# Rest of the layer: four of twelve norms scaled by VectorE, the fp8 overflow test in one operation, and the pieces of the four batches in another order

## The chip, the cores and the metric

The kernel runs on one core of a Trainium2 chip. The metric is the device time of one execution in microseconds; the median of several runs counts. TensorE does matmuls and transposes, VectorE and GpSimd elementwise work and reductions, ScalarE activations and copies, SyncE issues the transfers. Each engine works through its own list of instructions in the order in which it is written, and waits at semaphores.

## What is computed

One decoder layer on `x` (4 batches, 512 positions, 128 features) with a context of 77 rows. Each of three parts is added to its input and normalised:

```python
x = _layernorm(x + attn(x, Wq, Wk, Wv, bq, bk, bv, Wo, bo))       # causal, 16 heads of 64
x = _layernorm(x + xattn(x, ctx_1024, ctx_1024, Wq, Wk, Wv, Wo))  # 16 heads of 8, 77 keys
x = _layernorm(x + ffn(x, kernel, input_scale, kernel_scale, bias))
# _layernorm: (x - mean) / sqrt(var + 1e-5); ffn: x to bf16, / s_in, to float8_e4m3fn, one 128x128 matmul
```

In `float8_e4m3fn` a value that rounds to more than 448 becomes NaN. The kernel does this rounding in fp32 by hand.

## The kernel before

`self_attention` does the causal attention of all heads up to the product with Wo. It takes the first 319 us and is the same before and after. `rest_of_layer` does everything behind it, in pieces. A piece is a small function with a batch number, and each engine has its part of it under the same name. A piece's TensorE part fills a bank (or two banks) of PSUM, and another engine takes the result out:

- `y(b)`: attention times Wo, 32 matmuls. VectorE adds the input (`add(1, b)`) and takes mean and variance (`stats(1, b)`); then comes the norm.
- `t(b)`, `q(b)`: the normed batch transposed, and the queries from it; ScalarE copies both out, VectorE makes the low half (`q_lo`).
- `m(b, k)`, k from 0 to 7: scores in the other orientation, of which VectorE takes the maxima (tile `top`, line 850). `r(b)` transposes these maxima, ScalarE copies them to `shift`.
- `s(b, k)`, k from 0 to 3: the shifted scores of four heads, 16 matmuls into two places; ScalarE takes the exponentials in two halves (tile `p_t`, line 694, half 0 and then half 1).
- `p(b, part)`: exponentials times values, 8 matmuls (16 in the trace, which shows two passes for fp32). `o(b, part)`: transpose; VectorE divides (`o_n`). `u(b)`: transpose back. `z(b)`: times Wo.
- `add(2, b)`, `stats(2, b)`, norm; `cast(b)` on ScalarE (bf16, scale); `fp8(b)` on VectorE (rounding, `quant`); `x(b)`, `f(b)`: transpose and the feed-forward matmul; `add(3, b)`, `stats(3, b)`, norm, and SyncE stores the batch.

`s(1, 2)` is written s(1,2) below, and so on. `norm(l, b)` of GpSimd has two steps: the power -0.5 of the variance (tile `rstd`, line 755) and four scalings of 128x128 (line 758).

PSUM is shared by table `USES`: places n0 and n1 are one bank each, x0, x1 and x2 two banks each. The table lists for each place the pieces that use it, in order. `claim` lets TensorE start a piece only when the place's previous user has been taken. A piece `s(b,k)` needs two of the three x places; half 0 of its exponentials frees the first of them, half 1 the second. The order of the pieces on each engine is written out by hand, as a list of calls, in each engine's block. So TensorE, too, holds everything behind a piece that waits.

Of the kernel before, what the change touches and what calls it, by code (L numbers as in the profile page):

```python
# [440 lines left out]
def rest_of_layer(nc, banks, attn_t, consts, consts_in, x_nat, out):  # L441
# [7 lines left out]
    with ctx:  # L449
# [72 lines left out]
        @block.tensor
        def _(pe):
# [138 lines left out]
            x(1); f(1); x(2); f(2); x(3); f(3)

        @block.scalar
        def _(act):
# [71 lines left out]
            t(0); q(0); t(1); q(1); r(0); t(2); q(2); s(0, 0, 0); s(0, 0, 1); s(0, 1, 0); s(0, 1, 1); r(1); t(3)  # L737
            p(0, 0); s(0, 2, 0); s(0, 2, 1); q(3); s(0, 3, 0); s(0, 3, 1); s(1, 0, 0); s(1, 0, 1); p(0, 1)
            s(1, 1, 0); s(1, 1, 1); r(2); s(1, 2, 0); s(1, 2, 1); p(1, 0); s(2, 0, 0); s(2, 0, 1); u(0); s(1, 3, 0)
            s(1, 3, 1); s(2, 1, 0); p(1, 1); s(2, 1, 1); cast(0); u(1); s(2, 2, 0); r(3); s(2, 2, 1); p(2, 0)  # L740
            s(3, 0, 0); s(3, 0, 1); x(0); s(2, 3, 0); s(2, 3, 1); f(0); s(3, 1, 0); p(2, 1); cast(1); s(3, 1, 1)
# [229 lines left out]
```

## Time and profile before

| | us |
|---|---|
| median of 3 runs | 483.58 (483.56 to 483.71) |
| profiled execution | 480.95 |
| its span, first to last instruction | 479.2 |
| busy in the span: TensorE, VectorE, ScalarE, GpSimd | 413.8, 307.9, 254.3, 248.1 |
| granted clock of TensorE, mean | 0.932 |

The profiled execution is 2.6 us shorter than the median of the timed runs. Times inside the trace count from the start of the span. A granted clock of 1.00 is 2.4 GHz, 0.50 is 1.2 GHz, and a mean between them mixes the two. The share of busy time is over the whole span; the part that is changed begins at 319 us.

### The profile page before, as it was taken

The page shows a single profiled execution, that of the slowest core. Times are in us where ns is not written, and L with a number is a line of the kernel's source. Part 1 is how long each engine was busy: PE and PEld are TensorE (multiplying, and loading weights), DVE is VectorE, ACT ScalarE, POOL GpSimd, SP SyncE. Part 2 cuts the span into 40 slices and gives each one's busy share as a digit, 9 for nine tenths or more (in the row PEclk, how much of TensorE's full clock was granted, in tenths as well). Part 3 has the DMA queues.
Part 4 walks back from the last instruction along what each step waited for, and adds up shares of the span by engine and source line. Part 5 has one row for each costly group of instructions (what it writes and reads, how often), then busy time and mean ns, then how long its engine had stood idle before and what let it go on. Part 6 is the DMA issues. An engine that isn't in the chain of part 4 may idle for free. (4 is left out here: it accounts for less than half of the span.)

```text
span 479.2 us, 10059 instructions
## 1 busy us (share of the span) xinstructions
PE 413.8 (86%) x3954; PEld 291.1 (61%) x3954; DVE 307.9 (64%) x901; ACT 254.3 (53%) x370; POOL 248.1 (52%) x318
## 2 busy tenths in 40 slices
PE   3789999999999999999999999867998798787500
PEld 1576776777777677677677777547974334344200
DVE  1558878777877777877877777344248433566772
ACT  2266666667667667666766756511011447755410
POOL 2377856556646646655655664645642000335277
PEclk9899999999999999999999999999996679977955
DMA  7300000000000000000000000020000000000001
GB/s 248 98 2 1 1 3 1 2 1 1 1 2 3 0 2 4 0 1 1 2 1 1 3 1 1 1 83 6 1 2 0 1 0 1 1 0 23 1 22 45
DMA packets 4559, 6.89 MB, mean 14 GB/s; under 512 B 1440, under 2 KB 2976, under 8 KB 4384
## 3 DMA queue, kind: packets, MB, share of 16 engines
q1 hardware_dynamic: 4512, 6.24, 4.0%
q8 instruction: 32, 0.52, 0.5%
q14 instruction: 15, 0.12, 0.1%
HBM read 5.19 MB, written 1.05 MB: 13 GB/s over the span
## 5 line engine op out<-in xcount | busy, mean ns | idle before, releaser
L312 DVE CUSTOM_DVE_ANT_0 unused<-banks,neg_mask 128x512 bf16<-128x512 f32 (+3 forms) x256 | 112.6, 487 | 43.1 <-PE banks L108 43.0
L255 ACT ACTIVATE probs<-banks 128x768 f32<-128x768 f32 (+1 forms) x96 | 84.9, 884 | 56.5 <-PE banks L129 56.5
L370 POOL TENSOR_SCALAR_AFFINE_SELECT probs<-probs 128x256 f32<-128x256 f32 x128 | 50.5, 407 | 110.4 <-ACT probs L255 107.6
L158 PE MATMUL banks<-probs,v_nat 128*64 128x256 f32 (+3 forms) x512 | 74.4, 432 | 0.0
L158 PEld LDWEIGHTS banks<-probs,v_nat 128*64 128x64 f32 x512 | 37.0, 137 | 45.5 <-issue 40.4
L388 POOL TENSOR_TENSOR p_sum<-probs 128x768 f32<-128x768 f32 x32 | 58.6, 1830 | 2.7
L755 POOL TENSOR_TENSOR rstd<-var_e,halves 128x4 f32<-128x4 f32 x12 | 12.4, 1038 | 90.0 <-DVE var_e L834 90.0
L124 PE MATMUL banks<-q_hi,k_hi 64*128 64x512 f32 (+3 forms) x256 | 45.9, 354 | 2.9 <-ACT probs L255 2.9
L129 PE MATMUL banks<-shift,ones_r 64*128 64x512 f32 (+3 forms) x256 | 45.2, 348 | 0.0
L321 DVE SCALAR_TENSOR_TENSOR q_lo<-banks,bias_qk,q_hi 128x512 fp32r<-128x512 f32 x32 | 24.0, 751 | 29.6 <-ACT q_hi L277 29.6
L395 POOL TENSOR_TENSOR p_sum<-p_sum,probs 128x512 f32<-128x512 f32 x32 | 40.9, 1277 | 2.7
L124 PE MATMUL banks<-q_lo,k_hi 64*128 64x512 f32 (+3 forms) x256 | 41.6, 320 | 0.0
L124 PE MATMUL banks<-q_hi,k_lo 64*128 64x512 f32 (+3 forms) x256 | 41.5, 319 | 0.0
L261 ACT CAST shift<-banks 128x512 fp32r<-128x512 f32 x32 | 18.8, 587 | 40.0 <-PE banks L138 40.0
L108 PE MATMUL banks<-k_hi,q_hi 64*128 64x512 f32 (+3 forms) x256 | 37.3, 326 | 1.7 <-DMA attn_t<-w_qkv 1.7
L694 ACT ACTIVATE p_t<-banks 77x1024 f32<-77x1024 f32 x32 | 31.2, 1018 | 13.2 <-PE banks L606 13.2
L850 DVE TENSOR_REDUCE top<-banks 128x8 f32<-128x616 f32 x32 | 24.2, 795 | 19.2 <-PE banks L587 18.9
L200 PE MATMUL banks<-x_hi,w_hi 64*128 64x512 f32 x128 | 27.1, 417 | 7.1 <-POOL neg_max L402 6.2
L566 PE MATMUL banks<-wo_s,attn_t 128*128 128x128 f32 x256 | 29.4, 276 | 3.3 <-POOL vx L777 2.5
L338 DVE TENSOR_TENSOR banks<-banks,r_near 128x512 f32<-128x512 f32 x32 | 22.4, 700 | 14.4 <-ACT r_near L287 10.7
L129 PEld LDWEIGHTS banks<-shift,ones_r 64*128 64x128 f32 x256 | 24.4, 186 | 11.7 <-ACT shift L261 11.7
L566 PEld LDWEIGHTS banks<-wo_s,attn_t 128*128 128x128 f32 x256 | 28.8, 192 | 3.9 <-issue 2.7
(121 smaller groups left out, 881.1 us busy)
## 6 DMA issues: line engine op xcount, KB each, us to landing
attn_t<-w_qkv SPq DMA_DIRECT2D x1, 1344.0 KB, 8.1
attn_t<-xT SPq DMA_DIRECT2D x4, 256.0 KB, 8.5
x_s<-x_nat SPq DMA_DIRECT2D x1, 1024.0 KB, 5.8
out<-y_out SPq DMA_DIRECT2D x4, 256.0 KB, 2.0
...
```

Source lines behind the costliest of these rows:

```text
L108: last = mm(mx[:, h, at:at + n], q_hi[HALF[h], v % 3, i * T:(i + 1) * T], k_hi[HALF[h], v % 3, 0:n], start=True, stop=True)
L124: mm(st[:, h, at:at + n], k[HALF[h], par, ks], q[HALF[h], par, j * T:S], start=(c == 0), stop=False)
L129: last = mm(st[:, h, at:at + n], ones_r[HALF[h], :], shift[HALF[h], v % 2, j * T:S], start=False, stop=True)
L158: last = mm(o_ps[HALF[h], j * T:S], v_nat[:, v // 2 % 2, j, v % 2, HALF[h]], p_of(v, j, h, 0, S - j * T), start=(j == 0), stop=(j == NT - 1))
L200: last = mm(aux[qk], w[HALF[h], qk, p, :], x[HALF[h], xs], start=(part == 0 and c == 0), stop=(part == 1 and c == 2))
L255: nc.scalar.activation(probs[:, v % 2, AT[j]:AT[j] + 2 * n].rearrange("p (h s) -> p h s", h=2), st[:, :, 0:n], ACT.Exp, scale=D ** -0.5).t ...
L312: last = V.tensor_tensor_reduce(out=unused[:, h, at:at + n], in0=mx[:, h, at:at + n], in1=neg_mask[:, S - n:S], scale=-1.0, scalar=3.0e38, ...
L370: return nc.gpsimd.affine_select(out=blk, in_=blk, compare_op=ALU.is_ge, fill=0.0, base=0, pattern=pattern + [[1, T]], channel_multiplier=-1)
L388: nc.gpsimd.tensor_tensor(acc[:, :, :], heads(0, T, S), heads(1, 0, S - T), ALU.add).then_inc(added, 1)
L395: nc.gpsimd.tensor_tensor(acc[:, :, T:], acc[:, :, T:], heads(2, 0, 2 * T), ALU.add).then_inc(added, 1)
L566: last = mm(dst[:, i * T:(i + 1) * T], attn_t[:, p, at:at + T], wo_s[:, p, :], start=(p == 0), stop=(p == PAIRS - 1))
L694: nc.scalar.activation(p_t[:, k, 2 * half:2 * half + 2, :], place[bank][0:C, :, :], ACT.Exp, scale=DK ** -0.5).then_inc(taken[bank], 1)
```

## The change

Three edits, all in `rest_of_layer`.

1. The norm is split into `power(l, b)`, which stays on GpSimd, and `scale(l, b)`. Four of the twelve scalings, (1,0), (2,3), (3,2) and (3,3), are done by VectorE in the same form, four operations of 128x128; eight stay on GpSimd. Waits for a normed batch now ask the semaphore of the engine that scaled it.
2. `rounding` tested for overflow with three operations (square, compare and scale, scale to infinity times zero). Now one operation scales the value by 7.2e35 and multiplies by zero, which is NaN where the value was 480 or more. Each `fp8(b)` has six VectorE operations instead of eight.
3. The table of PSUM places and the lists of calls of all engines are in a new order.

```diff
 USES = {
-    "x0": "k m00 m03 m05 m11 m14 m17 m20 s01 m24 s02 m27 m31 m32 s11 m34 s20 s13 s21 s30 s23 s32 s33",
-    "x1": "v m01 m04 m07 m13 m16 s00 m21 m23 s02 s03 m30 s10 m33 s12 m35 s13 m37 s22 s23 s31 s33",
-    "x2": "m02 m10 m06 m12 m15 s00 s01 m22 m25 m26 s03 s10 s11 s12 s20 m36 s21 s22 s30 s31 s32",
+    "x0": "k m01 m04 m07 m14 m20 s00 m23 s01 m25 s03 m27 s11 m31 s13 s20 s21 m36 s22 s30 s31 s33",
+    "x1": "v m02 m05 m10 m12 m15 m21 m22 m17 m24 s02 m26 s10 m30 s12 s13 s20 m35 m37 s23 s30 s32 s33",
+    "x2": "m00 m03 m06 m11 m13 m16 s00 s01 s02 s03 s10 s11 s12 m32 m33 m34 s21 s22 s23 s31 s32",
 }
...
+        SCALED = {"pool": "11 12 13 20 21 22 30 31".split(), "dve": "10 23 32 33".split()}
...
+        def wait_scaled(eng, l, b):
+
+            by = "pool" if f"{l}{b}" in SCALED["pool"] else "dve"
+            eng.wait_ge(scaled[by], SCALED[by].index(f"{l}{b}") + 1)
...
-            norm(1, 0); norm(1, 1); norm(1, 2); norm(1, 3); norm(2, 0); norm(2, 1); norm(3, 0); norm(2, 2)
-            norm(2, 3); norm(3, 1); norm(3, 2); norm(3, 3)
+            power(1, 0); power(1, 1); scale(1, 1); power(1, 2); scale(1, 2); power(1, 3); scale(1, 3); power(2, 0)
+            scale(2, 0); power(2, 1); scale(2, 1); power(2, 2); scale(2, 2); power(3, 0); scale(3, 0); power(2, 3)
+            power(3, 1); scale(3, 1); power(3, 2); power(3, 3)
...
-                    lambda: V.tensor_tensor(m, v, v, ALU.mult),
-                    lambda: V.tensor_scalar(m, m, 448.0 ** 2, 3.0e38, ALU.is_gt, ALU.mult),
-                    lambda: V.tensor_scalar(m, m, 3.0e38, 0.0, ALU.mult, ALU.mult))
+                    lambda: V.tensor_scalar(m, v, 7.2e35, 0.0, ALU.mult, ALU.mult))
...
+            def scale(l, b):
+
+                dve.wait_ge(pow_out, POWS.index(f"{l}{b}") + 1)
+                for i in range(NT):
+                    last = V.tensor_scalar((y_out if l == 3 else xn)[:, b, i, :], r_s[:, b, i, :], mv[:, b, i, 0:1],
+                                           rstd[:, b, i:i + 1], ALU.subtract, ALU.mult)
+                last.then_inc(dve_scaled, 1)
```

In TensorE's list `y(3)` stood ahead of `q(0)` and all `m`; now `t(0)`, `t(1)`, `q(0)` and the first five `m` of batch 0 stand ahead of it. The next place is TensorE from the fourth part of `s(0,0)` on. The old list reads s(0,0) m(2,0) s(0,1) m(2,1) r(1) m(2,2) m(2,3) m(2,4) m(2,5) p(0,0) s(0,2); line 606 is `s`, 587 is `m`, 537 with `top` is `r`, 617 is `p`. Before, from the end of s(0,1):

```order
L606 MATMUL banks<-shift,neg_sel 77x512 x4
L587 MATMUL banks<-kx_hi,q_hi 128x308 x2
L537 MATMUL banks<-ident_f_s,top 128x128 x4
L587 MATMUL banks<-kx_hi,q_hi 128x308 x8
L617 MATMUL banks<-p_t,vx 32x512 x8
L606 MATMUL banks<-q_hi,kx_hi 77x512 x4
```

Now, at the same place; line 615 is `s`, 596 `m`, 546 with `top` is `r`, 626 is `p`:

```order
L615 MATMUL banks<-shift,neg_sel 77x512 x4
L596 MATMUL banks<-kx_hi,q_hi 128x308 x2
L546 MATMUL banks<-ident_f_s,top 128x128 x4
L615 MATMUL banks<-q_hi,kx_hi 77x512 x4
L615 MATMUL banks<-q_lo,kx_hi 77x512 x4
L615 MATMUL banks<-q_hi,kx_lo 77x512 x4
L615 MATMUL banks<-shift,neg_sel 77x512 x4
L596 MATMUL banks<-kx_hi,q_hi 128x308 x2
L626 MATMUL banks<-p_t,vx 32x512 x8
L615 MATMUL banks<-q_hi,kx_hi 77x512 x4
```

Between s(0,1) and s(0,2) there were five `m`, `r(1)` and `p(0,0)`; now there are one `m` and `r(1)`, and `p(0,0)` stands behind s(0,2).

The other place is VectorE at its end. The first rows are `add(2,3)` and `stats(2,3)`, then `add(3,1)`. Before:

```order
L816 TENSOR_TENSOR r_s<-banks,xn 128x512
L827 BN_STATS stats<-r_s 128x6 x4
L831 BN_AGGR mv<-stats 128x2 x4
L834 TENSOR_SCALAR var_e<-mv 128x4
L806 TENSOR_TENSOR xq<-y_b,ffn_b_s 128x512
L810 TENSOR_TENSOR r_s<-xq,xn 128x512
L827 BN_STATS stats<-r_s 128x6 x4
L831 BN_AGGR mv<-stats 128x2 x4
L834 TENSOR_SCALAR var_e<-mv 128x4
L806 TENSOR_TENSOR xq<-y_b,ffn_b_s 128x512
L810 TENSOR_TENSOR r_s<-xq,xn 128x512
L790 TENSOR_SCALAR qm<-qv 128x512
```

Now:

```order
L825 TENSOR_TENSOR r_s<-banks,xn 128x512
L836 BN_STATS stats<-r_s 128x6 x4
L840 BN_AGGR mv<-stats 128x2 x4
L843 TENSOR_SCALAR var_e<-mv 128x4
L815 TENSOR_TENSOR xq<-y_b,ffn_b_s 128x512
L819 TENSOR_TENSOR r_s<-xq,xn 128x512
L849 TENSOR_SCALAR xn<-r_s,mv,rstd 128x128 x4
L836 BN_STATS stats<-r_s 128x6 x4
L840 BN_AGGR mv<-stats 128x2 x4
L843 TENSOR_SCALAR var_e<-mv 128x4
L801 TENSOR_SCALAR qm<-qv 128x512
```

`scale(2,3)` (line 849) is new behind `add(3,1)`, and `add(3,2)` has moved behind `fp8(3)`. The last eight VectorE operations are now `scale(3,2)` and `scale(3,3)`.

## Rows read from the trace of the kernel before

**Rows 1.** The page's slices of the span: TensorE busy, and its granted clock.

```profile
PE   3789999999999999999999999867998798787500
...
PEclk9899999999999999999999999999996679977955
```

**Rows 2.** Stretches: us, busy time (instructions) of each engine, granted clock, DMA.

```profile
357.50:372.30 14.80, 12.57 (x51) 6.15 (x50) 12.61 (x23) 2.38 (x5) 4.15 (x5) 0.68 0.00 0
372.30:394.00 21.70, 17.68 (x117) 8.21 (x116) 9.13 (x13) 10.34 (x13) 0.00 (x0) 0.67 0.00 1
394.00:408.80 14.80, 13.04 (x146) 7.20 (x150) 6.56 (x12) 11.06 (x14) 0.00 (x0) 1.00 0.01 1
408.80:424.70 15.90, 13.34 (x106) 6.23 (x106) 8.08 (x21) 9.48 (x13) 4.16 (x5) 0.79 0.00 1
424.70:452.60 27.90, 19.88 (x168) 10.34 (x165) 18.98 (x55) 15.76 (x22) 13.41 (x15) 0.88 0.03 11
```

**Rows 3.** TensorE in order of time: start, us, line, operation [idle before, releaser].

```profile
333.32 14.53 PE L566 MATMUL banks<-wo_s,attn_t 128*128 128x128 f32 x128 [2.45 <-POOL vx L777]
...
348.63 7.41 PE L566 MATMUL banks<-wo_s,attn_t 128*128 128x128 f32 x64 [0.34 <-DVE r_s L816]
...
381.52 3.64 PE L617 MATMUL banks<-p_t,vx 77*32 77x512 f32 x16
385.09 0.71 PE L606 MATMUL banks<-q_hi,kx_hi 32*77 32x512 f32 x4
...
395.36 1.92 PE L617 MATMUL banks<-p_t,vx 77*32 77x512 f32 x16
397.36 0.47 PE L606 MATMUL banks<-q_hi,kx_hi 32*77 32x512 f32 x4
...
400.61 0.46 PE L606 MATMUL banks<-q_hi,kx_hi 32*77 32x512 f32 x4 [1.37 <-ACT p_t L694]
...
439.87 0.71 PE L606 MATMUL banks<-q_hi,kx_hi 32*77 32x512 f32 x4
...
449.38 1.16 PE L539 MATMUL banks<-w_x_s,on_t 128*128 128x128 f32 x8 [0.73 <-ACT on_t L671]
```

**Rows 4.** VectorE in order of time, the same columns.

```profile
358.21 7.15 DVE L850 TENSOR_REDUCE top<-banks 128x8 f32<-128x616 f32 x10
...
439.98 0.69 DVE L816 TENSOR_TENSOR r_s<-banks,xn 128x512 f32<-128x512 f32 x1 [1.65 <-PE banks L539]
...
452.60 0.68 DVE L816 TENSOR_TENSOR r_s<-banks,xn 128x512 f32<-128x512 f32 x1
...
461.23 0.43 DVE L790 TENSOR_SCALAR qm<-qv 128x512 int32<-128x512 int32 x1 [2.80 <-ACT qv L714]
...
463.87 0.82 DVE L794 TENSOR_TENSOR qm<-qv 128x512 f32<-128x512 f32 x1
...
465.65 0.69 DVE L877 TENSOR_TENSOR xq<-qv,qm 128x512 bf16<-128x512 f32 x1
...
469.17 0.51 DVE L806 TENSOR_TENSOR xq<-y_b,ffn_b_s 128x512 bf16<-128x512 bf16 x1 [1.43 <-ACT y_b L725]
...
471.81 0.18 DVE L834 TENSOR_SCALAR var_e<-mv 128x4 f32<-128x4 f32 x1
```

**Rows 5.** GpSimd in order of time, at the end.

```profile
456.13 3.67 POOL L758 TENSOR_SCALAR xn<-r_s,mv,rstd 128x128 f32<-128x128 f32 x4
...
472.56 1.02 POOL L755 TENSOR_TENSOR rstd<-var_e,halves 128x4 f32<-128x4 f32 x1
473.69 3.12 POOL L758 TENSOR_SCALAR y_out<-r_s,mv,rstd 128x128 f32<-128x128 f32 x4
```

**Rows 6.** ScalarE in order of time: two exponentials, and the last cast.

```profile
398.54 1.93 ACT L694 ACTIVATE p_t<-banks 77x1024 f32<-77x1024 f32 x2 [0.61 <-PE banks L606]
...
459.83 0.62 ACT L712 CAST x_b<-xn 128x512 bf16<-128x512 f32 x1 [3.24 <-POOL xn L758]
```

**Rows 7.** Tile qv: durations in ns, first and last start, form.

```profile
L790 DVE TENSOR_SCALAR qm<-qv x1: 227/227/227, 322.7 to 322.7; 128x128 int32<-128x128 int32 x1
```

More of the change, by code:

```diff
@@ L707, in cast @@
             def cast(b):
-                act.wait_ge(norm_out, norm_at(2, b) + 1)
+                wait_scaled(act, 2, b)
                 if b:
@@ L735, in _ @@
             act.wait_ge(prep, 2)
[L737 to L741, printed above, removed]
-            u(2); s(3, 2, 0); s(3, 2, 1); s(3, 3, 0); s(3, 3, 1); p(3, 0); p(3, 1); cast(2); u(3); x(1); f(1); x(2)
-            f(2); cast(3); x(3); f(3)
+            t(0); q(0); t(1); q(1); t(2); q(2); r(0); t(3); s(0, 0, 0); s(0, 0, 1); s(0, 1, 0); s(0, 1, 1); r(1)
+            s(0, 2, 0); s(0, 2, 1); p(0, 0); s(0, 3, 0); s(0, 3, 1); q(3); s(1, 0, 0); s(1, 0, 1); p(0, 1)
+            s(1, 1, 0); s(1, 1, 1); r(2); s(1, 2, 0); s(1, 2, 1); p(1, 0); u(0); s(1, 3, 0); s(1, 3, 1); s(2, 0, 0)
+            s(2, 0, 1); p(1, 1); s(2, 1, 0); s(2, 1, 1); cast(0); u(1); s(2, 2, 0); s(2, 2, 1); r(3); s(2, 3, 0)
+            s(2, 3, 1); p(2, 0); s(3, 0, 0); s(3, 0, 1); p(2, 1); cast(1); s(3, 1, 0); s(3, 1, 1); u(2); s(3, 2, 0)
+            x(0); s(3, 2, 1); s(3, 3, 0); s(3, 3, 1); p(3, 0); f(0); p(3, 1); cast(2); x(1); u(3); f(1); x(2); f(2)
+            cast(3); x(3); f(3)
         @block.gpsimd
@@ L749, in _, with power @@
             values = v2_s[:, :, :].rearrange("k b (t a d) -> k (b t) a d", t=8, a=2)
-            def norm(l, b):
-                n = norm_at(l, b)
-                pool.wait_ge(var_out, n + 1)
+            def power(l, b):
+                pool.wait_ge(var_out, norm_at(l, b) + 1)
                 P.tensor_tensor(rstd[:, b, :], var_e[:, b, :], halves[:, :], ALU.pow).then_inc(pow_out, 1)
-                pool.wait_ge(pow_out, n + 1)
+            def scale(l, b):
+                pool.wait_ge(pow_out, POWS.index(f"{l}{b}") + 1)
                 for i in range(NT):
@@ L759, in norm @@
                                            rstd[:, b, i:i + 1], ALU.subtract, ALU.mult)
-                last.then_inc(norm_out, 1)
+                last.then_inc(pool_scaled, 1)
             P.memset(halves[:, :], -0.5).then_inc(zeroed, 1)
@@ L834, in stats, with scale @@
                 V.tensor_scalar(var_e[:, b, :], mv[:, b, :, 1], EPS, None, ALU.add).then_inc(var_out, 1)
+            def scale(l, b):
+                dve.wait_ge(pow_out, POWS.index(f"{l}{b}") + 1)
[3 more added lines that the diff above has]
+                last.then_inc(dve_scaled, 1)
             def q(b):
@@ L899, in _ @@
             dve.wait_ge(zeroed, 2)
-            add(1, 0); stats(1, 0); add(1, 1); stats(1, 1); add(1, 2); stats(1, 2); add(1, 3); stats(1, 3); m(0, 0)
-            m(0, 1); m(0, 2); m(0, 3); m(1, 0); m(0, 4); m(0, 5); m(0, 6); m(0, 7); m(1, 1); q(0); m(1, 2); m(1, 3)
-            q(1); m(1, 4); m(1, 5); m(1, 6); m(1, 7); m(2, 0); q(2); m(2, 1); m(2, 2); m(2, 3); m(2, 4); m(2, 5)
-            m(2, 6); q(3); m(2, 7); m(3, 0); m(3, 1); o(0, 0); m(3, 2); m(3, 3); o(0, 1); m(3, 4); m(3, 5); o(1, 0)
-            m(3, 6); add(2, 0); stats(2, 0); m(3, 7); o(1, 1); fp8(0); add(2, 1); stats(2, 1); o(2, 0); add(3, 0)
-            stats(3, 0); o(2, 1); fp8(1); add(2, 2); stats(2, 2); o(3, 0); o(3, 1); fp8(2); add(2, 3); stats(2, 3)
-            add(3, 1); stats(3, 1); add(3, 2); fp8(3); stats(3, 2); add(3, 3); stats(3, 3)
+            add(1, 0); stats(1, 0); scale(1, 0); add(1, 1); stats(1, 1); add(1, 2); stats(1, 2); m(0, 0); m(0, 1)
+            m(0, 2); m(0, 3); m(0, 4); q(0); add(1, 3); stats(1, 3); m(0, 5); m(0, 6); m(1, 0); q(1); m(1, 1)
+            m(0, 7); m(1, 2); m(1, 3); m(1, 4); m(1, 5); m(2, 0); m(1, 6); q(2); m(2, 1); m(2, 2); m(2, 3); m(1, 7)
+            m(2, 4); m(2, 5); m(2, 6); o(0, 0); m(2, 7); q(3); m(3, 0); m(3, 1); o(0, 1); m(3, 2); m(3, 3)
+            add(2, 0); stats(2, 0); m(3, 4); o(1, 0); m(3, 5); o(1, 1); m(3, 6); m(3, 7); fp8(0); add(2, 1)
+            stats(2, 1); o(2, 0); o(2, 1); fp8(1); add(2, 2); stats(2, 2); add(3, 0); o(3, 0); stats(3, 0); o(3, 1)
+            fp8(2); add(2, 3); stats(2, 3); add(3, 1); scale(2, 3); stats(3, 1); fp8(3); add(3, 2); stats(3, 2)
+            add(3, 3); stats(3, 3); scale(3, 2); scale(3, 3)
 _INS = ["xT", "w_qkv", "b_qk", "b_v", "causal", "ident", "x_nat", "wo", "b_o", "ctx_t", "w_x", "row_mask",
```

30 lines of the change are left out of this document (16 added, 14 removed), and 4 rows, old and new, of the table USES.

## The prediction

> **What bounds the kernel now.** I read the page first, then stretches, then each engine in order of time. The page's slices [rows 1] show TensorE at nine tenths and a granted clock of 0.9 or more for the first 30 slices. Behind them both become ragged, and the last two slices have no TensorE work. So the changed part has two regimes: a middle, up to the last `z`, and a tail, in which one batch runs alone through all engines.
>
> The stretches [rows 2] say what holds the middle. From 357.5 to 372.3 VectorE is busy 12.61 of 14.80 us: it takes the maxima of `m`, 10 in 7.15 us, 0.72 each [rows 4]. From 372.3 no engine is full, except that TensorE looks busy, 17.68 of 21.70, at a granted clock of 0.67. At 1.00 (394.0 to 408.8) the same kind of work moves quickly. Two things therefore cost time here: pieces in the order in which they stand in a queue, and the low clock. The low level is dear: a `p` took 3.64 us at 381.5 and 1.92 us at 395.4 [rows 3].
>
> In the tail, read backwards [rows 4 to 6]: the last variance is ready at 471.99 (471.81 + 0.18), but GpSimd is still scaling batch 2 and starts its power at 472.56. The last scaling begins at 473.69. Before that, 3.67 us of GpSimd scaling of (2,3) from 456.13 stand directly in front of the cast at 459.83, and VectorE's `fp8(3)`, started at 461.23, ends at 466.34.
>
> **The change: the tail.** I count from the start of `add(2,3)`, 452.60, to the end of the span, 479.2: 26.6 us.
>
> - `scale(2,3)` on VectorE. No row shows this operation at this size with two scalars from memory. The nearest is a VectorE operation of 128x128 with constants, 0.227 us alone [rows 7]; four of them one behind another give 0.9 at most, and by the same row somewhat less if they overlap, as the ten `top` operations do. The upper bound is GpSimd's 3.67 [rows 5]. The operation is of VectorE's kind, so I take 0.75. It stands behind `add(3,1)` (about 1.2), which is as long as the power (1.02 and a hand-off) that it waits for. Saving: 3.67 - 0.75 = 2.9. Range of this term: 0 to 3.1.
> - `stats(3,1)` stands behind it, about 1.5, beside cast and scale on ScalarE (459.83 to 461.23, 1.4). It costs 0.1 or 0.2.
> - Overflow test. Three operations from 463.87 to 465.65, 1.78 us, become one of 0.46. Saving 1.3. The other three `fp8` save the same, behind which `add(2,1)`, `add(2,2)` and `add(2,3)` stand on VectorE; that is in the middle's count.
> - From the end of `fp8(3)` through `x(3)` and `f(3)` to 469.17 nothing changes, 2.8 us. `add(3,2)` and `stats(3,2)`, about 2.8 together, now fill just this gap; if they are longer by a few tenths, so is the tail.
> - The last norm. Before: 471.99 to 476.81 (473.69 + 3.12), 4.8 us. Now GpSimd has only powers left: 1.1 with its hand-off, during which VectorE does `scale(3,2)`, then `scale(3,3)`, 0.75. With hand-offs 2.0. Saving 2.8.
>
> Sum: -2.9 + 0.1 - 1.3 - 2.8 = **-6.9** us, a tail of 19.7.
>
> **The change: the middle.** From 333.3, where `y(1)` starts [rows 3], to 452.60 it lasts 119.3 us. I walked through the new lists with durations at full clock (`y` 7.3 us, `s` 1.2, `p` 1.9, `z` 1.2, a maximum 0.72, two exponentials 1.93 [rows 3, 4, 6]), each piece starting when its place is free, its input there and its queue at it. The checkpoints, before and in my walk (the stretches of rows 2 are cut at the starts of s(0,0), s(1,0) and s(2,1)):
>
> - `s(0,0)` starts at 372.3; 371.4. `y(3)` is 7.4 us of pure TensorE work [rows 3], and it now starts about 4.6 us later, at 353.2, behind five `m`. VectorE, which was idle during `y(3)`, takes five maxima (3.6 us) in that time, then `add(1,3)` and `stats(1,3)` (2.3). Both ways VectorE has done about 4.4 us of this work by 360.5, so the exchange is near zero by itself. From there it has 11 maxima and one `q_lo` to do: 360.5 + 2.3 + 7.9 + 0.7 = 371.4.
> - `s(1,0)` starts at 394.0; 384.8. A step from one `s` to the next that shares the place freed last is the matmuls, 1.18 (397.36 to the exponentials at 398.54), then both exponentials, 1.93: with hand-offs 3.24 us, as from 397.36 to 400.61 [rows 3, 6]. One that shares the place freed first saves one exponential, about 2.3. New table: four steps of 3.2 to 3.5, 13.4 us, where the trace has 21.7. The reason is in the queue: s(0,2) stood behind `p(0,0)` and five `m` and started at 385.09. VectorE and ScalarE waited meanwhile, and the clock was low.
> - `s(2,1)` starts at 408.8; 402.9. Here 3.3 us go back, since `p(1,1)` is now ahead of it (before, behind it).
> - `s(3,3)` starts at 439.87; 423.3. Steps of 3.8, 3.3, 3.0, 4.4, 3.6, 2.3. Before, TensorE here twice waited behind ScalarE, which waited for a GpSimd scaling ahead of a `cast`, and lost its clock twice. In my walk `cast(0)` finds its batch ready, at 405.6, before ScalarE comes to it.
> - `add(2,3)` starts at 452.60; 435.9. `z(3)` ends near 434.8 (at 450.5 before: 449.38 + 1.16), and `fp8(2)`, one us later, decides.
>
> At full clock this is -16.7. It is too good by two amounts. The walk leaves out hand-offs of some 0.1 us where two engines finish together: I add 1.5. And it assumes the clock. Before, rows 2 show means of 0.68, 0.67, 0.79 and 0.88. With two levels, 1.00 and 0.50, that is (1 - mean)/0.5 of each stretch at the low one: 9.5, 14.3, 6.7 and 6.7, together 37 us. TensorE is busy for 0.8 of it, and low clock takes 0.47 of such time (1.92 instead of 3.64 for a `p`): 14 us at most. I take 12, since VectorE's maxima cover part of the first. The low passages came behind ones in which TensorE was idle or half idle. Its work in rows 2 is 76.5 us in 95.1, at full clock 64; the walk puts it, with 3 us of `y(3)`, into 78 us, so a share of 0.86 instead of 0.67. But it has the same VectorE-bound passage before s(0,0), three-microsecond steps with single `m` between them, and a thin end around `u(3)`, `z(3)`. I expect half of the loss to remain, 6 us. Middle: -16.7 + 1.5 + 6 = **-9.2**.
>
> On this the page "TensorE: Matmul & The Clock Gate", section "A second HAM failure mode: psum-queue depth-cycling", speaks against the change. By that section of the Trainium skill, a TensorE that idles briefly between groups while PSUM places are cycled makes its clock swing again and again. Place x2 is used by seven `s` in a row, so by that rule the loss would remain whole. Against it, this trace kept 1.00 from 394.0 to 408.8 [rows 2] in steps of 3.3 us with the same wait at each.
>
> **Sum.** -6.9 - 9.2 = -16.1. The profiled execution, 480.95, would be 464.8; its distance to the median (2.6) kept, 467.4: I say 467.4.
>
> **The rivals.**
>
> - A, chance 0.50: as above. Its own range is 463.5 to 471.5, half to nearly all of the clock loss either way and 1 us for the scaling term.
> - B, 0.17: the clock falls as often as before. TensorE work at 1.2 GHz costs the full 12: 467.4 + 6 = 473.4. For it speaks the same VectorE-bound stretch, against it the denser queue.
> - C, 0.18: the clock holds nearly throughout: 467.4 - 6 = 461.4. For it speaks 394.0 to 408.8, against it the mean of 0.79 right behind.
> - D, 0.09: the new order gives nothing, since what s(0,2) gains is given back at `cast` and `fp8` (the two chains per batch take the time that they take). Then only the tail counts: 483.6 - 6.9 = 476.7. Against it: the last of these chains, batch 2's, began at 439.98 with `add(2,2)`, which had waited 1.65 us for `z(2)` of TensorE [rows 4], at low clock.
> - E, 0.03, slower: TensorE stays at 1.2 GHz from `y(3)` on. It has to wait there for the maxima of the first `m`, and before, the clock fell in just such a passage (357.5 to 372.3, 0.68). `y(3)` would take 7 us more. The 54 us of TensorE work behind s(0,0) (63.9 by rows 2, less its share of the 12) would take 1.7 times as long, 92 us where the walk has 64: 28 more. With C's 461.4 that is 496. It decides once low clock costs more than 22 us, that is for some 50 of these 64. Before, the low passages of rows 2 added up to 28 of 80.
> - F, 0.03: a cancelling mix within 0.2%, which is about what a measurement of this kernel can tell from no change.
>
> **How the numbers follow.** The range 460 to 475 holds A, B and C almost whole, 0.82 with their outer edges cut; D and E lie outside. Faster by over 0.2% is A, B, C and D, 0.94; same 0.03; slower 0.03. If the VectorE scaling were as slow as GpSimd's, A would be at 472, still inside.
>
> **What would show it.** VectorE's four scalings of a batch at 0.6 to 0.9 us together, no L794 to L796 work but one operation of 0.43, `fp8(3)` at 3.5 to 3.9 us. A span of about 463, in it from `add(2,3)` to the end 19 to 20.5 us. s(0,0) at 371 to 375, s(0,2) within 7.5 us behind it, s(3,3) near 427, `add(2,3)` near 443. The mean granted clock over 357 to 443 above 0.80, with passages at 0.50 after thin ones. I am wrong if s(0,0) is later than 376 (then moving `y(3)` cost something), if steps between `s` exceed 4 us on average from s(0,0) to s(3,3), or if the tail is over 22.

## The result, and the profile after

The changed kernel takes 463.63 us (median of 4 runs, 458.4 to 467.37) against 483.57 for the kernel before; the ratio is 0.9566, 95% interval 0.9475 to 0.9657. In a second comparison it was 461.76 us (7 runs) and 0.9516 (0.9461 to 0.9571). The forecast was 467.4 in a range of 460 to 475. The profiled execution of the changed kernel is one of its longer ones, 467.37 us, and the comparison of the ratio leaves such executions out; I therefore read a second trace as well (trace 2, 467.75 us), and show where the length comes from.

The stretches of the changed kernel, columns as in [rows 2]:

```profile
357.50:372.30 14.80, 13.13 (x91) 9.57 (x91) 9.58 (x21) 1.68 (x3) 5.75 (x8) 0.94 0.00 1
372.30:394.00 21.70, 18.22 (x122) 8.66 (x118) 10.38 (x16) 9.95 (x14) 0.00 (x0) 0.66 0.00 1
394.00:408.80 14.80, 13.18 (x124) 6.70 (x125) 5.41 (x9) 9.52 (x14) 0.00 (x0) 0.87 0.00 1
408.80:424.70 15.90, 14.66 (x160) 7.31 (x162) 11.93 (x35) 12.71 (x17) 5.78 (x7) 1.00 0.00 1
424.70:439.00 14.30, 11.82 (x124) 5.92 (x116) 8.58 (x24) 10.81 (x15) 6.24 (x8) 1.00 0.01 1
439.00:465.60 26.60, 7.26 (x44) 4.76 (x40) 22.47 (x79) 7.50 (x12) 15.02 (x15) 0.56 0.11 41
```

Against [rows 2] the low clock is gone from 408.8 to 439.0. It is still there from 372 to 394, 0.66 where it was 0.67, and from 394.0 to 408.8 the clock is 0.87 where it was 1.00. In the last stretch TensorE works for 7 us only.

TensorE in order of time, columns as in [rows 3]: `y(3)`, s(0,0), s(0,1), s(0,2), p(0,0), s(1,0) and s(3,3).

```profile
357.86 7.41 PE L575 MATMUL banks<-wo_s,attn_t 128*128 128x128 f32 x64
...
376.87 0.46 PE L615 MATMUL banks<-q_hi,kx_hi 32*77 32x512 f32 x4 [0.18 <-DVE top L867]
...
380.43 0.56 PE L615 MATMUL banks<-q_hi,kx_hi 32*77 32x512 f32 x4 [0.64 <-DVE top L867]
...
384.37 0.71 PE L615 MATMUL banks<-q_hi,kx_hi 32*77 32x512 f32 x4 [0.81 <-ACT p_t L703]
...
386.56 3.64 PE L626 MATMUL banks<-p_t,vx 77*32 77x512 f32 x16
...
394.23 0.71 PE L615 MATMUL banks<-q_hi,kx_hi 32*77 32x512 f32 x4 [0.81 <-ACT p_t L703]
...
433.04 0.47 PE L615 MATMUL banks<-q_hi,kx_hi 32*77 32x512 f32 x4 [0.16 <-ACT p_t L703]
```

s(0,2) now comes 3.94 us behind s(0,1). `p(0,0)` follows it and still pays the low clock, 3.64 us.

VectorE in the tail, columns as in [rows 4]: `add(2,3)`, `scale(2,3)`, first and last operation of `fp8(3)` with the new test (line 805) between them, `add(3,3)`, and the last two scalings, `scale(3,2)` and `scale(3,3)`. Then GpSimd's last two powers.

```profile
445.66 0.69 DVE L825 TENSOR_TENSOR r_s<-banks,xn 128x512 f32<-128x512 f32 x1
...
449.12 1.11 DVE L849 TENSOR_SCALAR xn<-r_s,mv,rstd 128x128 f32<-128x128 f32 x4 [0.20 <-POOL rstd L762]
...
451.67 0.43 DVE L801 TENSOR_SCALAR qm<-qv 128x512 int32<-128x512 int32 x1
...
454.18 0.56 DVE L805 TENSOR_SCALAR qm<-qv 128x512 f32<-128x512 f32 x1
454.78 0.69 DVE L894 TENSOR_TENSOR xq<-qv,qm 128x512 bf16<-128x512 f32 x1
...
458.29 0.43 DVE L815 TENSOR_TENSOR xq<-y_b,ffn_b_s 128x512 bf16<-128x512 bf16 x1 [0.18 <-ACT y_b L734]
...
460.87 2.35 DVE L849 TENSOR_SCALAR y_out<-r_s,mv,rstd 128x128 f32<-128x128 f32 x8
```

```profile
458.19 1.03 POOL L762 TENSOR_TENSOR rstd<-var_e,halves 128x4 f32<-128x4 f32 x1 [0.94 <-DVE var_e L843]
461.04 1.03 POOL L762 TENSOR_TENSOR rstd<-var_e,halves 128x4 f32<-128x4 f32 x1 [1.82 <-DVE var_e L843]
```

The scaling of (2,3) takes 1.11 us where GpSimd took 3.67 [rows 5]. GpSimd is free for the last power at once, and the scalings end at 463.2, 2.25 us behind the last variance at 460.97; before it was 4.8.

All traces are compared by one table. Each number is the us between two starts read from the two timelines: t(0), s(0,0), s(1,0), s(2,1), s(3,3), `add(2,3)`, and the end of the span. The walk is that of the prediction, all at 1.00. The names of the other versions are those of the experiments below.

```
                    t00-s00  s00-s10  s10-s21  s21-s33  s33-add23  tail   span
before                24.6     21.8     14.7     31.1     12.7     26.6   479.2
walk                  23.7     13.4     18.1     20.4     12.6     19.7   455.6
changed, trace 1      24.6     17.4     18.6     20.2     12.6     19.9   465.6
changed, trace 2      28.8     18.6     17.2     20.2     12.8     20.0   465.0
order only            24.6     14.2     17.2     22.1     14.4     26.8   466.4
scalings only         24.6     21.7     14.7     31.1     12.7     22.4   476.1
fp8 test only         24.6     21.8     14.7     31.1     11.5     25.4   476.5
y3_early              32.5     18.6     20.5     20.2     12.5     20.0   471.8
p_ahead               24.7     18.0     17.2     20.2     12.5     20.0   461.6
m_twice               26.9     16.2     17.7     20.2     12.8     20.0   466.6
m_twice_early         27.0     15.8     17.2     20.2     12.5     20.0   465.1
filler_one            27.6     16.3     17.6     20.2     12.4     20.0   467.0
filler_two            31.2     14.7     17.9     20.2     12.5     20.0   465.3
filler_bf16           29.9     18.7     22.6     20.2     12.4     19.9   476.9
filler_bf16_late      29.1     14.7     17.4     20.2     12.4     19.9   464.0
```

The three columns from s(2,1) to the end repeat to 0.4 us in all versions with the new order and both other edits; what varies lies ahead of s(2,1). The granted clock varies there too: between s(0,0) and s(1,0) it is 0.67 before, 0.61 and 0.54 in the two traces of the changed kernel, 0.88 in order_only and 0.72 in p_ahead.

### The profile page after: what moved, and what is told of

Read it like the earlier page. It is cut to its first block and busy times, and to the rows that moved or that the text cites. A ratio compares the mean times of both kernels' runs of the same rounds, so it can differ in the third digit from the quotient of the medians.

```text
span 465.6 us, 10048 instructions
## 1 busy us (share of the span) xinstructions
PE 412.6 (89%) x3954; PEld 291.8 (63%) x3954; DVE 307.1 (66%) x907; ACT 253.9 (55%) x370; POOL 236.8 (51%) x302
## 5 line engine op out<-in xcount | busy, mean ns | idle before, releaser
L158 PE MATMUL banks<-probs,v_nat 128*64 128x256 f32 (+3 forms) x512 | 75.8, 438 | 0.0
L108 PE MATMUL banks<-k_hi,q_hi 64*128 64x512 f32 (+3 forms) x256 | 37.1, 326 | 1.5 <-ACT k_hi L277 1.5
L575 PE MATMUL banks<-wo_s,attn_t 128*128 128x128 f32 x256 | 30.9, 285 | 3.0 <-POOL vx L787 2.5
L338 DVE TENSOR_TENSOR banks<-banks,r_near 128x512 f32<-128x512 f32 x32 | 22.4, 700 | 16.1 <-ACT r_near L287 12.1
L575 PEld LDWEIGHTS banks<-wo_s,attn_t 128*128 128x128 f32 x256 | 30.4, 200 | 3.5 <-issue 2.7
L129 PEld LDWEIGHTS banks<-shift,ones_r 64*128 64x128 f32 x256 | 24.7, 189 | 11.5 <-ACT shift L261 11.4
```

Source lines behind the costliest of these rows:

```text
L108: last = mm(mx[:, h, at:at + n], q_hi[HALF[h], v % 3, i * T:(i + 1) * T], k_hi[HALF[h], v % 3, 0:n], start=True, stop=True)
L129: last = mm(st[:, h, at:at + n], ones_r[HALF[h], :], shift[HALF[h], v % 2, j * T:S], start=False, stop=True)
L158: last = mm(o_ps[HALF[h], j * T:S], v_nat[:, v // 2 % 2, j, v % 2, HALF[h]], p_of(v, j, h, 0, S - j * T), start=(j == 0), stop=(j == NT - 1))
L575: last = mm(dst[:, i * T:(i + 1) * T], attn_t[:, p, at:at + T], wo_s[:, p, :], start=(p == 0), stop=(p == PAIRS - 1))
```

## The experiments

**The three edits apart.** The new order and places with all scalings on GpSimd and the old test (first diff, the lists of calls and the test left out); the old order with four scalings on VectorE (second, only VectorE's last calls); the old kernel with the new test (third).

```diff
-        SCALED = {"pool": "11 12 13 20 21 22 30 31".split(), "dve": "10 23 32 33".split()}
+        SCALED = {"pool": "10 11 12 13 20 21 22 30 23 31 32 33".split(), "dve": []}
```
```diff
-            add(3, 1); stats(3, 1); add(3, 2); fp8(3); stats(3, 2); add(3, 3); stats(3, 3)
+            add(3, 1); scale(2, 3); stats(3, 1); add(3, 2); fp8(3); stats(3, 2); add(3, 3); stats(3, 3)
+            scale(3, 2); scale(3, 3)
```
```diff
-                    lambda: V.tensor_tensor(m, v, v, ALU.mult),
-                    lambda: V.tensor_scalar(m, m, 448.0 ** 2, 3.0e38, ALU.is_gt, ALU.mult),
-                    lambda: V.tensor_scalar(m, m, 3.0e38, 0.0, ALU.mult, ALU.mult))
+                    lambda: V.tensor_scalar(m, v, 7.2e35, 0.0, ALU.mult, ALU.mult))
```

> The changed kernel, but all twelve scalings on GpSimd right behind their powers and the overflow test in three operations: only the new places and lists remain. My theory, that order and tail edits add: the tail keeps its old length (26 us instead of 20) and fp8(2) holds add(2,3) 1.2 us longer, so 463.6 + 6.9 + 1.3 = 472. Rival, that the order alone gives nearly everything, since the scalings and the test hide behind other work: 464 to 466. Rival, that the order gives nothing: 476 or more.

Measured: 474.60 us, ratio 0.9759 (0.9687 to 0.9831), which is 471.9 on 483.6. The rival of the order giving all is out, and so is that of the order giving nothing (476 or more), the latter by half a microsecond at the near end of the interval. In the trace, which is of the shortest of the six executions (468.23 us), the tail is 26.8 us, as long as before (26.6).

> The kernel before in its old order, with the same four scalings moved to VectorE (scale(1,0) behind stats(1,0), scale(2,3) behind add(3,1), scale(3,2) and scale(3,3) last). My theory: 2.9 less for scale(2,3), 2.8 less at the last norm, minus some tenths for VectorE's scaling being 1.1 instead of 0.75 us: 483.6 - 5.0 = 478.6. Rival, that the scalings are covered: 483 to 484. Rival, that VectorE's added work delays the rounding behind it: 484 or more.

Measured: 478.29 us, ratio 0.9886 (0.9837 to 0.9935), 478.1 on 483.6. Of the columns only the tail changes, 26.6 to 22.4. The scalings on VectorE in this kernel, and between them `add(3,2)` and the first operation of `fp8(3)`:

```profile
457.16 1.11 DVE L850 TENSOR_SCALAR xn<-r_s,mv,rstd 128x128 f32<-128x128 f32 x4 [0.20 <-POOL rstd L761]
...
459.58 0.42 DVE L816 TENSOR_TENSOR xq<-y_b,ffn_b_s 128x512 bf16<-128x512 bf16 x1
460.04 0.69 DVE L820 TENSOR_TENSOR r_s<-xq,xn 128x512 f32<-128x512 bf16 x1
460.65 0.42 DVE L800 TENSOR_SCALAR qm<-qv 128x512 int32<-128x512 int32 x1
...
471.28 2.35 DVE L850 TENSOR_SCALAR y_out<-r_s,mv,rstd 128x128 f32<-128x128 f32 x8
```

`add(3,2)`, 1.1 us, stands directly in front of `fp8(3)` here, with no idle time. So `fp8(3)` starts 6.95 us behind `add(2,3)`; in the changed kernel, where the new order has `add(3,2)` behind it, it starts 6.01 us behind (445.66 to 451.67).

> The kernel before with only the overflow test in one operation instead of three. My theory: fp8(3) is on the tail's chain (1.3) and fp8(2) holds add(2,3) (1.2): 483.6 - 2.5 = 481.1. Rival, that only the last one counts: 482.3. Rival, that VectorE has slack everywhere: 483.5.

Measured: 478.92 us, ratio 0.9899 (0.9863 to 0.9934), 477.0 to 480.4 on 483.6. The trace shows the two steps expected, 1.2 us ahead of `add(2,3)` and 1.2 in the tail, with the rest of the table unchanged. The measured gain, 3.2 to 6.6 us, is larger than those 2.4 by 0.8 us even at the near end of its interval; no column shows where this comes from, and I leave it open. The expected 481.1 lies outside the interval.

The product of the three ratios is 0.9550, against 0.9566 and 0.9516 for the whole change. Within the intervals, 0.4 to 0.7% each, the edits add. The table shows more finely that the two smaller ones are worth more in the new order: from s(2,1) to the end order_only takes 63.3 us and the changed kernel 52.8, 10.5 less, while in the old order they gave 4.2 and 2.4, together 6.6. One part is `add(3,2)`: moving it saves nothing while the cast waits for GpSimd (the tail of order_only), and 0.9 us once `scale(2,3)` is on VectorE. Another is that the lists are tighter: in the old order `add(2,1)` waits 3.17 us for `z(1)` behind `fp8(0)`, so a shorter `fp8(0)` gains nothing there, while in order_only it starts at once, the scaling of (2,1) holds `cast(1)` for 2.01 us, and in the changed kernel for 0.87. The rest is not taken apart.

```profile
424.72 0.69 DVE L816 TENSOR_TENSOR r_s<-banks,xn 128x512 f32<-128x512 f32 x1 [3.17 <-PE banks L539]
```

```profile
418.76 0.62 ACT L721 CAST x_b<-xn 128x512 bf16<-128x512 f32 x1 [2.01 <-POOL xn L768]
```

```profile
427.29 0.62 ACT L721 CAST x_b<-xn 128x512 bf16<-128x512 f32 x1 [0.87 <-POOL xn L768]
```

The first line is of the kernel before, the second of order_only, the third of the changed kernel.

**The changed kernel again,** for its scatter.

> The changed kernel once more, to see how its executions scatter and to read a second trace. If the scatter of 458 to 467 us is the clock's, then a trace that is shorter than the first (span 465.6, mean clock 0.942) has a higher mean clock and the same tail from add(2,3) on, 19.9 us, and the difference lies in stretches with a granted clock below 1. If it is not the clock, the tail or VectorE's operations differ too.

Measured: 461.76 us (459.67 to 467.75). The second trace is again of a longer execution, span 465.0, so neither trace shows a typical one; but the span and the mean clock of all 11 executions are known. Spans of 455.9 to 458.3 us have 0.957 or 0.964, spans of 460.0 to 461.7 have 0.949 to 0.957, and spans of 465.0 to 465.9 have 0.938 to 0.942. With (1 - clock) / 0.5 of the span as time at the low level, 33 to 58 us of it, a straight line through the 11 executions gives 0.37 us of span for each us at the low clock (correlation 0.92). The median span is 460.1. The tails of the two traces are 19.9 and 20.0, as the clock theory wanted.

The two traces also show how it happens. Trace 1 reaches t(0) 4.6 us later than before, 3.0 of it already at the end of the unchanged attention and 1.6 in `y(1)` and `y(2)`, with a clock of 0.57 from 336 to 340. Trace 2 had its first fall behind `q(0)`: from 350 to 352 TensorE worked for 0.57 of 2 us, since it waited for ScalarE's copy of the queries and for the first maxima, and `y(3)`, which now follows, ran largely at the low level, 10.23 us where it takes 7.41. Stretches of trace 1, then of trace 2:

```profile
345.00:357.00 12.00, 10.13 (x85) 8.84 (x84) 5.26 (x22) 1.66 (x3) 6.23 (x8) 1.00 0.00 1
357.00:372.00 15.00, 13.06 (x92) 9.52 (x91) 9.78 (x22) 1.38 (x3) 6.25 (x8) 0.95 0.00 1
...
394.00:410.00 16.00, 14.38 (x136) 7.65 (x140) 6.29 (x11) 10.44 (x14) 0.00 (x0) 0.88 0.00 1
```

```profile
345.00:357.00 12.00, 9.83 (x61) 8.05 (x60) 6.34 (x16) 1.66 (x3) 6.21 (x8) 0.81 0.01 1
350.00:352.00 2.00, 0.57 (x9) 0.31 (x8) 0.87 (x2) 1.07 (x2) 1.90 (x3) 1.00 0.00 0
352.00:354.00 2.00, 1.70 (x7) 1.21 (x8) 2.00 (x4) 0.00 (x0) 2.00 (x3) 0.59 0.00 0
...
357.00:372.00 15.00, 13.27 (x81) 9.59 (x79) 8.36 (x19) 2.15 (x4) 4.15 (x5) 0.84 0.00 0
...
394.00:410.00 16.00, 13.63 (x148) 7.65 (x148) 7.33 (x15) 11.00 (x14) 0.00 (x0) 1.00 0.00 1
```

And `y(3)` in trace 2:

```profile
353.25 10.23 PE L575 MATMUL banks<-wo_s,attn_t 128*128 128x128 f32 x64
```

**y(3) ahead of the first maxima.**

```diff
-            y(1); y(2); t(0); t(1); q(0); m(0, 0); m(0, 1); m(0, 2); m(0, 3); m(0, 4); y(3); q(1); t(2); m(0, 5)
+            y(1); y(2); t(0); t(1); q(0); y(3); m(0, 0); m(0, 1); m(0, 2); m(0, 3); m(0, 4); q(1); t(2); m(0, 5)
```

On VectorE, `add(1, 3); stats(1, 3)` move ahead of `m(0, 0)` too.

> The changed kernel with y(3) moved ahead of the first five m on TensorE (behind q(0), which it needs), and add(1,3), stats(1,3) ahead of their maxima on VectorE. The walk through the lists: VectorE then idles for all of y(3) and has 16 maxima behind it, s(0,0) about 2.6 us later, 466. Rival, that this exchange is worth nothing, as VectorE's work is the same: 463 to 464. Rival, that a full TensorE with y(3) earlier changes the clock only: a few us either way and s(0,0) not later at full clock.

Measured: 475.58 us, ratio 0.9846 (0.9816 to 0.9876): 12 to 14 us slower than the medians of the changed kernel, not 2.6. VectorE shows two holes, and TensorE one:

```profile
358.65 0.69 DVE L825 TENSOR_TENSOR r_s<-banks,x_s 128x512 f32<-128x512 f32 x1 [8.72 <-PE banks L575]
...
368.63 2.41 DVE L867 TENSOR_REDUCE top<-banks 128x8 f32<-128x616 f32 x3 [3.64 <-PE banks L596]
```

```profile
365.14 2.04 PE L587 MATMUL banks<-x_t,w_x_s 128*128 128x512 f32 x2 [2.33 <-DVE q_lo L858]
```

The first hole of 8.72 us is `y(3)`, in which no maxima are ready. The second I had not seen: `q(1)` needs the bank that `q_lo(0)` empties, and that stands on VectorE behind five maxima. With `y(3)` behind the five `m`, all this happens during `y(3)`. Here TensorE stands for 2.33 us and then runs `q(1)` in 2.04 us where 1.02 is its time at full clock. s(0,0) is 32.5 us behind t(0) rather than 24.6 or 28.8, and the clock is 0.50 from 372 to 394 and 0.60 from 394 to 410. How much of the loss is the wait and how much the clock is not taken apart; all six executions have a mean clock of 0.917 to 0.935, below the lowest of the changed kernel (0.938).

**p(0,0) ahead of s(0,2).**

```diff
-            m(2, 0); m(2, 1); q(3); s(0, 0); m(2, 2); m(2, 3); m(1, 7); s(0, 1); m(2, 4); r(1); s(0, 2); m(2, 5)
-            p(0, 0); s(0, 3); m(2, 6); o(0, 0); s(1, 0); m(2, 7); p(0, 1); s(1, 1); m(3, 0); r(2); s(1, 2); m(3, 1)
+            m(2, 0); m(2, 1); q(3); s(0, 0); m(2, 2); m(2, 3); m(1, 7); s(0, 1); m(2, 4); r(1); p(0, 0); s(0, 2); m(2, 5)
+            s(0, 3); m(2, 6); o(0, 0); s(1, 0); m(2, 7); p(0, 1); s(1, 1); m(3, 0); r(2); s(1, 2); m(3, 1)
```

ScalarE's copy for `p(0,0)` moves ahead of the exponentials of s(0,2) too.

> The changed kernel with one piece in the old relation: p(0,0) ahead of s(0,2) instead of behind it, on TensorE and ScalarE. Theory that the place in TensorE's queue made s(0,2) late before: s(0,2) starts 2.4 us later at full clock, about 4 at the low one, and nothing gives it back, 466 to 468. Rival, that s(0,2) is held by its places and the exponentials and later slack absorbs the rest: 462 to 464.

Measured: 469.82 us, ratio 0.9665 (0.9610 to 0.9720), 467.4 on 483.6. Its interval does not meet that of the changed kernel in the second comparison, but overlaps the upper end of the first (0.9475 to 0.9657). TensorE at s(0,1), p(0,0), s(0,2), s(0,3):

```profile
377.18 0.71 PE L615 MATMUL banks<-q_hi,kx_hi 32*77 32x512 f32 x4 [0.64 <-DVE top L867]
...
381.76 1.92 PE L626 MATMUL banks<-p_t,vx 77*32 77x512 f32 x16 [1.28 <-ACT shift L680]
383.61 0.51 PE L615 MATMUL banks<-q_hi,kx_hi 32*77 32x512 f32 x4
...
387.51 0.71 PE L615 MATMUL banks<-q_hi,kx_hi 32*77 32x512 f32 x4 [1.85 <-ACT p_t L703]
```

The step from s(0,1) to s(0,2) is 6.43 us instead of 3.94, 2.5 more, as expected. But the next step gives most of it back in this trace: s(0,3) follows in 3.90 us instead of 5.76, as `p(0,0)` is no longer in between. From s(0,1) to s(0,3) it is 10.33 us at a mean clock of 0.67. With `p(0,0)` behind s(0,2) the same way took 9.70 and 9.86 us at 0.51 and 0.50 (changed kernel), 8.44 at 0.60 (m_twice_early) and 7.33 at 0.77 (order_only). So the place of one piece in TensorE's queue costs 0.5 us over the two steps against traces with a lower clock, and 1.9 and 3.0 against those two. By the ratios the kernel is 5 to 7 us slower than the changed one; its trace, of the shortest of the six executions, does not show where all of that lies.

**Can the clock be held?** In two kernels the matmuls of `m` are issued twice, for all batches (m_twice) or for batches 0 and 1 (m_twice_early, shown).

```diff
-                for g in (2 * part, 2 * part + 1):
+                for g in (2 * part, 2 * part + 1) * (2 if b < 2 else 1):
```

> The changed kernel with the two matmuls of every piece m issued twice into the same place, which adds TensorE work (0.25 us at full clock, 32 times) and changes no result. Theory, that the changed kernel still loses 4 to 7 us to the low clock between t(0) and s(1,0), and that it falls because TensorE is thinly used there: the time from t(0) to s(0,0) goes from 24.6 to 28.8 us in the traces so far to 24.5 to 26, and the kernel takes 459 to 461 in spite of the added 8 us of TensorE work. Rival, that the place of a piece in TensorE's queue is all that counts: each m between two s is 0.25 us later, some 16 of them count, 466 to 468. Rival, no effect: 462 to 464.

Measured: 467.63 us, ratio 0.9693 (0.9647 to 0.9739). The time is the one that the queue's rival gave, but the trace does not show its cause: from s(1,0) on this kernel is within 0.7 us of the two traces of the changed one, not some 4 us behind, and t(0) to s(0,0) takes 26.9 us at a mean clock of 0.84. The clock theory is not borne out; why the time is 4 to 6 us longer stays open.

> As before, but only the pieces m of batches 0 and 1 are issued twice, which all but one stand ahead of s(0,0), where VectorE's maxima at 0.72 us set the pace and the doubled m of 0.5 us still fits. Clock theory: t(0) to s(0,0) at 24.5 to 26 us, 460 to 462, and nothing lost later. If the queue is all that counts, 463 to 464, as TensorE has slack there.

Measured: 463.29 us, ratio 0.9565 (0.9516 to 0.9614), no different from the changed kernel. Its clock fell behind a stretch in which TensorE was busy for 2.88 of 4 us, and stayed low although TensorE was then busy nearly all the time, with `m` and with matmuls over all 128 rows (`q`, `r`, `t`):

```profile
366.00:370.00 4.00, 2.88 (x25) 1.62 (x24) 3.87 (x14) 1.17 (x2) 2.02 (x3) 1.00 0.00 0
370.00:374.00 4.00, 3.92 (x16) 1.79 (x17) 3.12 (x6) 0.59 (x1) 2.15 (x3) 0.54 0.00 0
374.00:378.00 4.00, 3.74 (x20) 2.25 (x20) 2.76 (x5) 1.17 (x2) 0.00 (x0) 0.50 0.00 0
```

So twice the matmuls of `m`, which use 32 rows, did not keep it. Next, matmuls whose result is not used (fillers), over all 128 rows, ahead of each `m` of batches 0 to 2, one or two, in fp32:

```diff
+                for fill in range(2 if b < 3 else 0):
+                    mm(dst[:, fill % 2, 0:T], wo_s[:, 0, :], id_f[:, :], start=True, stop=True)
```

> The changed kernel with one idle matmul over all 128 rows (128x128 by 128x128 in fp32, 0.23 us at full clock, result overwritten) ahead of each piece m of batches 0 to 2. The doubled m of 32 rows did not keep the clock up. Theory: it is a full-width matmul that counts as activity, so the clock falls more rarely between t(0) and s(1,0); s(0,0) at 24.5 to 25.5 us behind t(0), granted clock over that stretch above 0.9, 458 to 460. Rival: any added TensorE work there only delays, since the clock falls anyway: 463 to 466 with the clock at 0.94 to 0.96 over the whole.

Measured: 467.89 us, ratio 0.9690 (0.9641 to 0.9739). The clock was 1.00 from t(0) to s(0,0), which took 27.6 us all the same, and 0.79 from there to s(1,0).

> The same with two such matmuls, so that a piece m takes 0.7 us of TensorE, as long as its maximum on VectorE. Theory of the clock: it holds from t(0) to s(1,0), time 457 to 460. Rival that only delays: TensorE becomes the limit in that passage and the time is 466 or more.

Measured: 468.03 us, ratio 0.9694 (0.9634 to 0.9754). Stretches of filler_two:

```profile
347.00:372.00 25.00, 23.87 (x166) 18.87 (x165) 12.74 (x32) 2.83 (x5) 9.82 (x12) 1.00 0.00 1
372.00:394.00 22.00, 21.33 (x172) 13.06 (x170) 10.74 (x15) 9.93 (x13) 0.00 (x0) 1.00 0.00 1
394.00:410.00 16.00, 14.07 (x146) 7.73 (x148) 7.38 (x14) 10.96 (x14) 0.00 (x0) 1.00 0.01 2
410.00:440.00 30.00, 25.90 (x270) 12.37 (x262) 20.62 (x63) 23.29 (x31) 13.00 (x15) 1.00 0.00 1
```

Both theories had half of it. The clock was held, 1.00 all the way to 440, and the mean clocks of the six executions, 0.961 to 0.972, are at or above the highest of the changed kernel (0.964); s(0,0) to s(1,0) took 14.7 us instead of 17.4 or 18.6. But an `m` with two fillers takes 0.98 us of TensorE, more than VectorE's 0.72, and t(0) to s(0,0) took 31.2. The gain is eaten by its price. (The expectation of the next kernel says that the fp32 matmuls held 1.00 from 347 to 440. That holds with two of them ahead of each `m`, not with one.)

Cheaper fillers, two in bf16 (0.21 us together), ahead of all those `m`, or not ahead of the five in front of `y(3)`:

```diff
+                for fill in range(2 if (b, k) > (0, 4) and b < 3 else 0):
+                    mm(dst[:, fill % 2, 0:T], id_b[:, :], id_b[:, :], start=True, stop=True)
```

> The changed kernel with two idle bf16 matmuls of 128x128 by 128x128 ahead of each piece m of batches 0 to 2, results overwritten. The fp32 ones held the clock (1.00 from 347 to 440) but made an m cost 0.76 or 0.98 us of TensorE, more than VectorE's 0.72. If two of bf16 cost about 0.15 us together, an m stays at 0.45 to 0.55 and s(0,0) comes 25 to 26 us behind t(0). If that is still enough activity, the clock holds and the kernel takes 457 to 460, below the changed kernel; if it is too little, the clock falls as without them and the time is 463 to 465.

Measured: 476.83 us (464.22 to 478.73, mean clock 0.967 in the shortest execution, 0.921 to 0.928 in the others).

> The same, but not ahead of the five m that stand ahead of y(3), so that y(3) starts no later. If the falls of the clock behind y(3) are what costs, 457 to 460 and below the variant with all; if the fall ahead of y(3) matters too (one trace of two of the changed kernel had it), the scatter stays, 458 to 467.

Measured: 466.93 us, ratio 0.9649 (0.9603 to 0.9694). Neither holds the clock: 0.56 from 370 to 380 in the first and 0.50 in the second. The second takes 14.7 us from s(0,0) to s(1,0) at 0.91, as filler_two, but 29.1 to get to s(0,0). No version here beats the changed kernel.

## Why the prediction was right, and where its terms were off

**The tail** was forecast at 19.7 us for 26.6 and came out at 19.9 and 20.0. Inside it the VectorE scaling was under-sized: 1.11 us where the text took 0.75 from [rows 7]. That row has constants as scalars; with two scalars read from memory one operation takes 344 ns, not 227. The price of GpSimd was the other end of that term's range, and VectorE's is far nearer to the lower end. The last norm takes 2.25 us, where 2.0 was forecast, for the same reason. The 0.9 us that come from `add(3,2)` behind `fp8(3)` had been placed there by the prediction and not priced; scale_only shows them. `fp8(3)` runs from 451.67 to 455.47, 3.8 us, in the range of 3.5 to 3.9; the test in it takes 0.56 us, not 0.46.

**The middle** was forecast at -9.2 and came out, from t(0) to `add(2,3)`, at 93.4 and 97.6 for 104.9, so -11.5 and -7.3; from `y(1)`, where the forecast starts, it is -10.0 and -7.4. Point by point by the checkpoints: behind s(1,0) the walk says 18.1, 20.4 and 12.6, the two traces 18.6 or 17.2, 20.2, and 12.6 or 12.8. The reason given for the second of these numbers, 20.4 where it was 31.1, that the waits at `cast` go away, fits it for one of the two waits that it names, and no experiment undid it by itself. Before, `cast(0)` waited 1.91 us for GpSimd, and TensorE 2.01 us behind it; now it does not wait. But `cast(1)` came at 431.81, straight behind a copy that ended at 431.75. ScalarE did not wait for GpSimd there; TensorE's 1.79 us were spent on ScalarE's own cast, scaling and exponential, and the prediction was wrong about this wait. The kernel before, ScalarE and TensorE at the first wait, then at the second:

```profile
415.43 0.62 ACT L712 CAST x_b<-xn 128x512 bf16<-128x512 f32 x1 [1.91 <-POOL xn L758]
417.41 3.64 PE L617 MATMUL banks<-p_t,vx 77*32 77x512 f32 x16 [2.01 <-ACT on_t L671]
...
431.81 0.62 ACT L712 CAST x_b<-xn 128x512 bf16<-128x512 f32 x1
434.24 0.57 PE L606 MATMUL banks<-q_hi,kx_hi 32*77 32x512 f32 x4 [1.79 <-ACT p_t L694]
```

Ahead of s(1,0) the walk is at 37.1, the traces at 42.0 and 47.4: 4.9 and 10.3 us more, where the prediction added 7.5 for the clock and the hand-offs together. That this is the low clock is read from the granted clock of these stretches; order_only, at 0.93 and 0.88, is at 38.8. Trace 1 lost a further 4.6 us ahead of t(0), where TensorE's list is the same as before. Behind s(1,0) the sums are 51.4 and 50.2 for 51.1 in the walk, so nothing had to be added there: the correction of 7.5 lies between the two traces' losses and was placed too wide. `z(3)` did run at the low level, 2.08 us for 1.16, but it ends when `fp8(2)` does in trace 1 and holds `add(2,3)` for 0.24 us in trace 2.

**The sum** is in part luck. The walk's span is 455.6 and the forecast's 463.1, while the changed kernel's executions spread from 455.9 to 465.9 with a median of 460.1, and the two that were traced are of the three longest. In a typical execution some 4.5 of the 7.5 us are lost, then, and no trace shows where. The distance between the profiled execution and the median, 2.6 us added before, has no reason to repeat and did not: the profiled executions are 3.7 and 6.0 us longer than their medians. That the traces, at 467.4 and 467.8, hit the forecast of the median is luck; the medians, 463.63 and 461.76, are 3.8 and 5.6 below it.

**The signs of being wrong.** One of the three was met: s(0,0) came at 376.87 and 376.23, later than 376. In trace 1 that is the late t(0), and the way from t(0) is 24.6 us as before. In trace 2 it is what the sign was meant for: the move put a thinly used passage in front of `y(3)`, the clock fell in it, and `y(3)` took 2.8 us more. The prediction had that only as rival E. The steps from s(0,0) to s(3,3) are 3.7 us on average in both traces, and the tail is 20. The scalings, forecast at 0.6 to 0.9 us, take 1.11; s(0,2) comes 7.5 and 8.7 us behind s(0,0), for at most 7.5.

**The reason for the first batch's gain** was given as the queue: `p(0,0)` and five `m` in front of s(0,2). The runs bear it out as far as they go. The changed kernel takes 17.4 and 18.6 us from s(0,0) to s(1,0) for 21.8, though its clock there is lower (0.61 and 0.54 for 0.67). The order alone, at 0.88, has 14.2 us, against 13.4 in the walk. Putting only `p(0,0)` back costs 2.5 us at its step and 0.5 to 3 over two. The other part, the five `m`, was not undone by itself.

**The exchange at y(3)** was called near zero by itself, compared with the old list. Trace 1 and order_only agree: 24.6 us from t(0) to s(0,0), as before. Trace 2, with 28.8, does not. Inside the new list it is not a free choice: the other way round costs 12 to 14 us, and its trace shows the coupling of `q(1)` to `q_lo(0)`, which the walk had not worked out for that case, and a low clock.

**The rule on the clock.** The Trainium skill ("TensorE: Matmul & The Clock Gate", section "A second HAM failure mode: psum-queue depth-cycling") tells of another kernel, in bf16, in which TensorE idles briefly between groups while PSUM places are cycled and its clock goes back and forth. Taken as a rule, it would have had the falls remain in every batch. They did in the first, 0.66 from 372 to 394. From 408.8 to 439 both traces stay at 1.00, with PSUM places in the same rotation.

Of the rivals, B (all clock losses remain, 473.4) lies above every execution (458.4 to 467.8). C (no clock loss, 461.4) has a number near the medians, 463.63 and 461.76, but four executions lie below it and its cause is not what the traces show, as the clock is 0.61 and 0.54 from s(0,0) to s(1,0). D is refuted by order_only, E and F by every execution.
